# Pair counts in 256-wide items, the typed layers each in one block, the clone search moved into the first product

## The reference

```python
edge_index = jnp.stack([src, dst])
x = _layernorm(x + arma2(x, edge_index))          # L0: two ARMA convolutions of 3 stacks, batch norm, relu
x = _layernorm(x + gcn(x, edge_index))            # L1: D^-1/2 (A+I) D^-1/2 (x W) + b
x = _layernorm(x + rgcn(edge_index, edge_type_9, x))   # L2: below, two layers
x = _layernorm(x + (segment_sum(x[src], dst) @ W_neigh.T + b_neigh) + (x @ W_self.T + b_self))   # L3
# L2, per layer:
agg = segment_sum(output[srcs], seg, 2 * R * n).reshape(2 * R, n, -1)   # seg: (type, direction, node)
hidden = output @ W[-1] + b[-1]
for r in range(R):
    for inv in (0, 1):
        s = r + R * inv
        hidden = 2.0 * (hidden + agg[s] @ W[s] + count[s] * b[s]) / cnt[s]
```

## Time and profile before

| | |
|---|---|
| median of 3 runs | 4263.36 us (4261.74 to 4271.8) |
| profiled execution | 4261.65 us, span 4260.4 us |
| PE | 3151.3 us busy, 74% of the span |
| PEld | 2507.9 us, 59% |
| DVE | 2177.2 us, 51% |
| POOL | 1996.6 us, 47% |
| ACT | 1410.3 us, 33% |
| DMA | 572.7 MB moved, mean 134 GB/s |

### The profile page before, as it was taken

The page is one execution under the profiler, slowest core; times in us unless marked ns, Lnnn a source line. Parts: engine busy times, 40 slices in busy tenths (PEclk is TensorE's granted clock), DMA queues, the critical chain, the costliest instruction groups (busy, mean ns, idle before and its releaser), DMA issues. The chain is left out here.

```text
span 4260.4 us, 54185 instructions
## 1 busy us (share of the span) xinstructions
PE 3151.3 (74%) x15552; PEld 2507.9 (59%) x15554; DVE 2177.2 (51%) x3834; ACT 1410.3 (33%) x2732; POOL 1996.6 (47%) x2227
## 2 busy tenths in 40 slices
PE   6878665899999799998966878767683544444459
PEld 3545322779999596996735767655552533333348
DVE  8979996425544651556655555434363422222224
ACT  5949575556666663665200000000000000000015
POOL 4727221111111010110276777777756777777751
PEclk8989898999999899999985565555586855555559
DMA  4000156558888392984562222222263222222226
GB/s 168 5 1 1 51 200 200 204 191 293 290 290 286 136 309 92 315 286 175 197 235 67 54 54 53 53 53 54 53 242 122 53 53 53 53 53 53 53 67 209
DMA packets 170983, 572.68 MB, mean 134 GB/s; under 512 B 54368, under 2 KB 63937, under 8 KB 170380
## 3 DMA queue, kind: packets, MB, share of 16 engines
q1 hardware_dynamic: 90838, 396.53, 27.1%
q0 software_dynamic: 79536, 172.73, 14.0%
q10 hardware_dynamic: 390, 0.60, 0.0%
HBM read 405.92 MB, written 163.77 MB: 134 GB/s over the span
## 5 line engine op out<-in xcount | busy, mean ns | idle before, releaser
L2070 PE MATMUL ps_sum_rgcn<-gathered_rgcn,select_sum_rgcn 128*128 x3328 | 971.1, 439 | 570.3 <-SPq L1961 513.5
L2070 PEld LDWEIGHTS ps_sum_rgcn<-gathered_rgcn,select_sum_rgcn 128*128 128x128 f32 x3328 | 760.3, 307 | 637.0 <-issue 635.5
L1650 PE MATMUL ps_sum_arma<-pair_counts_f_sum_arma,parts_sum_arma 128*128 128x448 f32 (+1 forms) x3850 | 852.3, 373 | 14.3 <-ACT pair_counts_f_sum_arma L1691 13.6
L1986 POOL DMA_INDIRECT gathered_rgcn<-by_dst,row x782 | 739.1, 945 | 238.3 <-issue 214.9
L1650 PEld LDWEIGHTS ps_sum_arma<-pair_counts_f_sum_arma,parts_sum_arma 128*128 128x128 f32 x3850 | 708.3, 190 | 68.4 <-issue 15.1
L1986 POOL DMA_INDIRECT gathered_rgcn<-by_src,row x558 | 527.3, 945 | 199.4 <-issue 156.0
L2107 ACT COPY acc_rgcn<-ps_sum_rgcn 128x128 f32<-128x128 f32 x100 | 26.6, 266 | 1640.3 <-PE ps_sum_rgcn L2070 1640.3
L1529 POOL DMA_DIRECT2D rows<-parts_sum_arma x275 | 152.5, 555 | 884.9 <-DVE parts_sum_arma L1738 840.6
L2144 DVE TENSOR_TENSOR select_sum_rgcn<-one_hot_sum_rgcn,ps_coef_sum_rgcn 128x2048 f32<-128x2048 bf16 x52 | 118.9, 2287 | 575.6 <-PE ps_sum_rgcn L2070 575.5
L531 POOL DMA_INDIRECT scattered_rows<-record_sorts,to_row_sorts x254 | 244.0, 960 | 191.0 <-POOLq L199 114.2
L1995 PE MATMUL ps_turn_sum_rgcn<-ident,one_hot_sum_rgcn 128*128 128x128 bf16 x832 | 244.3, 301 | 79.3 <-DVE one_hot_sum_rgcn L2116 51.6
(11 more groups left out here) (466 smaller groups left out, 5132.5 us busy)
## 6 DMA issues: line engine op xcount, KB each, us to landing
blocks_arma_mid<-pairs SPq DMA_DIRECT2D x125, 800.0 KB, 6.3
axT_arma<-pairs SPq DMA_DIRECT2D x100, 800.0 KB, 6.2
pair_counts_arma_sum<-pairs SPq DMA_DIRECT2D x50, 800.0 KB, 6.2
rows<-parts_sum_arma POOLq DMA_DIRECT2D x275, 128.0 KB, 5.5
by_src<-rows_rgcn_tables SPq DMA_DIRECT2D x50, 576.0 KB, 3.8
by_dst<-rows_rgcn_tables SPq DMA_DIRECT2D x50, 576.0 KB, 3.6
exact<-whole_pairs SPq DMA_DIRECT2D x25, 800.0 KB, 3.3
pairs<-whole_pairs POOLq DMA_DIRECT2D x25, 800.0 KB, 5.2
```

Of the source, the lines that this page charges most:

```text
L1650: last = nc.tensor.matmul(ps[:, g, 0:here.stop - here.start], half(part), counts[:, n % 2, here].bitcast(F32R), start=t == 0 and part == 0 ...
L1986: nc.gpsimd.indirect_dma_start(got[:, n % PLACES, :], None, table, bass.IndirectOffsetOnAxis(ap=o.row[:, n % C:n % C + 1], axis=0)).then_i ...
L2070: nc.tensor.matmul(ps[:, bass.ds(slot, P)], select[:, parity, u, :], rows[:, bass.ds(place, D)], start=False, stop=False, skip_group_check ...
```

## The change

- *Load.* x is loaded under its own semaphore, which the ranking's SP waits for before its fill of `by_src`; only the last tile of x is zeroed; the stores of blank rows move from SP's to ScalarE's queue; `row_of` is written by VectorE; the iotas `steps` and `spare_row` move to GpSimd in the ranking.
- *Staircase.* Blocks of 256 targets (REACH), 13 a tile, 728 items, three rounds of 128 blocks; the limits are worked out for rooms of four blocks. The heavy and clone search goes. SP stores `dinv_loop` here, and the block waits for it.
- *Pair counts.* TensorE's loop is written out; it loads 16 registers per fourteen items and waits per seven; VectorE waits per eight. ScalarE casts and clears 1024 columns, a clear right after its own cast. The block waits for no store; SP fetches the first four tiles of the half counts into the ring of the first product, whose buffers and the output buffers lie in a stage around both.
- *First product.* Four tiles are fetched before; later fetches wait for the tile's store. The heavy nodes are found on VectorE at tile 2, the clone rows at tile 4, the marks in five parts at tiles 5 to 9, the nodes at tile 11; GpSimd gathers the clone rows after storing its row 11, when all count stores have landed; the subtraction is at tile 14, the factors start at tile 14.
- *Typed layers.* Tables and sum stand in one block (and layer 0's turn back in layer 1's block). Table rows and the sum's select, turned and mine buffers share SBUF, the PSUM banks are shared; VectorE waits for all table stores before its first select; GpSimd's gathers run on without EARLY, and wait for all tables at the first row of the second. SP loads the next layer's weights behind the tables.

The diff, cut to its core:

```diff
@@ load_stage
-            nc.vector.memset(k.xcur[:, :, :], 0.0).then_inc(zeroed, 1)
-            nc.vector.memset(k.row_of[:, :, :], 0.0).then_inc(cleared, 1)
+            nc.vector.memset(k.xcur[:, NT - 1, :], 0.0).then_inc(zeroed, 1)
+            nc.vector.memset(k.row_of[:, :, :], 0.0)
...
+            for first in (0, LOW):
+                here = slice(first, first + NT)
+                nc.vector.tensor_copy(k.row_of[here, :, :], k.ident16[here, here, None].to_broadcast([NT, NT, P]))
@@ rank_stage
+            @block.gpsimd
+            def _(gp):
+                nc.gpsimd.iota(k.steps[:, :, :], [[1, C], [0, 2]], base=0, channel_multiplier=0,
...
+                sp.wait_ge(k.x_loaded, 32)
@@ pair_counts_stage
             for n in range(ITEMS):
-                dve.wait_ge(multiplied, n + 1)
+                if n % EIGHT == 0:
+                    dve.wait_ge(multiplied, n + EIGHT)
...
-            with pe.Fori(0, ITEMS // BODY) as i:
...
+            for n in range(ITEMS):
+                if n % FOURTEEN == 0:
+                    table = load(PE, item_at, n // FOURTEEN * ROW, ROW, (RUNS - 1) * REACH)
+                    frees = [value & COUNTS for value in table[FOURTEEN:ROW]]
+                if n % SEVEN == 0:
+                    pe.wait_ge(made, n + SEVEN)
+                    pe.wait_ge(freed, frees[n % FOURTEEN // SEVEN])
+                    nc.tensor.nop(nofuse=True)
+                nc.tensor.matmul(ps[:, bass.ds(table[n % FOURTEEN], REACH)], source[:, n // V % 2, n % V // 2, :, n % 2],
+                                 target[:, n % V, :], start=False, stop=False, skip_group_check=True).then_inc(multiplied, 1)
...
-                    if i or g:
-                        clear(i * SPANS + g - 1)
+                    if i < NT - 1:
+                        clear(i * ROOMS + g)
...
-            for n in (0, 1):
-                sp.wait_ge(stored[n], 16 * len(range(n, NT, 2)))
-                sp.wait_ge(kept[n], 16 * len(range(n, NT, 2)))
+                if J <= i < J + FETCHED:
+                    n = i - J
+                    sp.wait_ge(kept[n % 2], 16 * (n // 2 + 1))
+                    sp.dma_start(ring[:, n, :], halves[n * P:n * P + P, :]).then_inc(k.prefetched, 16)
@@ dense_stage
+                    if exact is not None and t == NODED:
+                        gp.wait_ge(noded, 1)
+                        for n in (0, 1):
+                            gp.wait_ge(k.exact_kept[n], 16 * len(range(n, NT, 2)))
+                            gp.wait_ge(k.kept[n], 16 * len(range(n, NT, 2)))
...
+                if exact is not None and n == READY:
+                    heavy_nodes()
+                if exact is not None and n == COUNTED:
+                    clone_rows()
+                if exact is not None and FILLED <= n < FILLED + TURNS:
+                    clone_marks(n - FILLED)
+                if exact is not None and n == NODED:
+                    clone_nodes()
+                if exact is not None and n == RESTED:
                     dve.wait_ge(k.cloned, 32)
@@ typed_tables_stage, typed_sum_stage -> typed_layer_stage
-            gp.wait_ge(tiled, NT)
-            for n in range(BEHIND, EARLY):
-                gather(n)
...
+            gp.wait_ge(tiled, NT)
+            for n in range(BEHIND, TOTAL * U):
                 if not fetched(n):
                     continue
+                if n == C:
+                    gp.wait_ge(tiled, TILES)
...
+            for j in range(J):
+                dve.wait_ge(stored[j], 16 * (TILES // J))
@@ rgcn_layer
-        for layer, xT in ((0, k.xT[:, :]), (1, hidden)):
-            typed_tables_stage(nc, k, f"rgcn_tables{layer}", xT, [dram["by_src"], dram["by_dst"]], got, acc)
-            typed_sum_stage(nc, k, f"sum_rgcn{layer}", typed, got, acc, layer == 0,
-                            loads=() if layer else typed_loads(k, A, 1))
-            turn_back_stage(nc, k, f"rgcn_back{layer}", acc, hidden, ACT.Copy if layer else ACT.Relu)
+        typed_layer_stage(nc, k, "sum_rgcn0", k.xT[:, :], tables, got, acc, True, loads=typed_loads(k, A, 1))
+        typed_layer_stage(nc, k, "sum_rgcn1", hidden, tables, got, acc, False, turned_from=ACT.Relu)
+        turn_back_stage(nc, k, "rgcn_back1", acc, hidden, ACT.Copy)
```

More of the change, by code:

```diff
@@ L1037, in staircase_stage, with _ @@
         block = c.block()
+        @block.sync
+        def _(sp):
+            with nc.allow_non_contiguous_dma(reason="one value per node"):
+                sp.dma_start(loop.rearrange("(t p) o -> p (t o)", p=P), k.dinv_loop[:, :]).then_inc(looped, 16)
+            sp.wait_ge(looped, 16)
         @block.gpsimd
         def _(gp):
-            nc.gpsimd.iota(after_iota[:, :], [[1, P]], base=1, channel_multiplier=0,
-                           allow_small_or_imprecise_dtypes=True)
             nc.gpsimd.iota(at[:, :], [[1, ITEMS]], base=0, channel_multiplier=0,
@@ L1078, in _ @@
             last.then_inc(laid, 1)
-            pe.wait_ge(reached, 1)
-            nc.tensor.matmul(ps[0:1, 4, P:P + U], row[:, :], k.ident[0:U, 0:U], start=True, stop=True).then_inc(lined, 1)
-            pe.wait_ge(cloned, 1)
-            for t in range(NT):
-                last = nc.tensor.matmul(ps[:, 5, 2 * LOW:2 * LOW + 2], clone[:, t, :], place[:, t, :], start=(t == 0),
-                                        stop=(t == NT - 1))
-            last.then_inc(placed, 1)
         @block.scalar
@@ L1659, in _ @@
                         last.then_inc(used, 1)
+                if exact is not None and n == COUNTED - 1:
+                    pe.wait_ge(ready, 1)
+                    nc.tensor.transpose(ps[0:U, 7, 0:P], lane_rows[:, :], k.ident[:, :])
+                    nc.tensor.matmul(ps[:, 7, TWO_P:TWO_P + NT], ones[:, :], heavy16[:, :], start=True, stop=True)
+                    nc.tensor.matmul(ps[:, 7, TWO_P + LOW:TWO_P + LOW + NT], before[:, :], heavy16[:, :], start=True,
+                                     stop=True).then_inc(counted, 1)
+                if exact is not None and n == NODED - 1:
+                    pe.wait_ge(filled, 1)
+                    nc.tensor.matmul(ps[0:1, 7, P:P + U], row[:, :], k.ident[0:U, 0:U], start=True, stop=True)
+                    for u in range(NT):
+                        last = nc.tensor.matmul(ps[:, 7, TWO_P + 2 * LOW:TWO_P + 2 * LOW + 2], clone[:, u, :], place[:, u, :],
+                                                start=(u == 0), stop=(u == NT - 1))
+                    last.then_inc(placed, 1)
                 if loops and t < NT - 1:
@@ L1687, in _ @@
                     head(m)
[L1688 removed]
+                wait_streamed(act, n)
                 if n >= 2:
```

545 lines of the change are left out of this document (284 added, 261 removed).

## The result

The changed kernel takes 4298.94 us (median of 4 runs, 4292.98 to 4302.73) against 4263.23: ratio 1.0078, interval 1.0061 to 1.0096. It is slower by 0.8%; the forecast was 4223, 1% faster, range 4202 to 4250. The profiled execution took 4302.73 us, 41.1 more than that of before.

| stage | before | after | difference | forecast |
|---|---|---|---|---|
| load | 14.3 | 13.0 | -1.3 | -4.5 |
| first ranking | 34.8 | 39.4 | +4.6 | +4.5 |
| first sort | 174.0 | 184.1 | +10.1 | 0 |
| its end | 7.4 | 8.6 | +1.2 | 0 |
| degrees and second sort | 191.1 | 191.0 | 0.0 | 0 |

The account below looks back on a forecast made before the run. No engine was above 74% busy, so waits at block ends were taken as the bound. Typed layers -30.4, pair counts -1, first product -9, staircase +1 and load 0 took 4261.65 to 4222, stated as 4223 us; range 4202 to 4250.

Parts of the forecast that it names:

- The typed layers: Both layers: one block removes GpSimd's switch gaps and its waits for the sum's matmuls, -30.4 us, bounds -22 to -34.
- the second wait: Layer 0's sum: GpSimd's 9.00 us wait for matmuls, expected to vanish; its return would leave the typed layers at -22.
- The first product: First product: 14.6 us of waits and stall go, about 6 us of clone search is exposed; -9, bounds -15 to -4.
- Staircase: Staircase: a third threshold round, more columns and longer picks, less the clone chain and eight tail steps; +1 us.
- Load and ranking: Load and first ranking: load gains 3 to 6 us, iotas cost the ranking 0 to 5.2; net 0, bounds -6 to +5.
- Pair counts: Pair counts: narrower compares gain nothing, TensorE adds 6.4 us, the tail saves 7.5; together -1, bounds -15 to +21.
- VectorE's new wait: Pair counts: once in eight compares VectorE waits for matmuls at least eight back, with nothing behind but compares; no cost given.
- a whole register load: Pair counts, TensorE: the shortest pause, 0.84 us, was read as holding a full load; 1.0 us was taken per fourteen matmuls.
- The prediction's own sign of being wrong: Pair counts: a pause over 1.8 us per fourteen matmuls was named among the signs that would show the forecast wrong.
- Rival 4: Pair counts: written-out TensorE at half clock, pauses over 2 us per fourteen; 262 us there, 4276 in all; chance 0.04.
- The tail: End of pair counts: without waiting for stores, last compare to next block falls from 13.1 to about 5.6 us, -7.5.
- The clock: Pair counts, TensorE: granted clock between 0.55 and 0.95; 200 us at full, 218 at half, the middle 209 taken, +6.4.

## Why the prediction was wrong

- *The typed layers* (-30.4): right in mechanism and size, -33.2. The gaps gone give 30.4 between the first and the last gather of the layers (999.1 to 978.9 and 988.7 to 978.5), where 29.4 was said, and the switch 2.5 where 1.0 was said. The feared return of the second wait did not come.
- *The first product* (-9): right, -9.5; the stall came at tile 14 as placed, and its 5.67 us are near the 6 that were taken for all that was added. (The 4.27 and 10.60 that go make 14.9, not 14.6.)
- *Staircase* (+1): 1.1 came, but by luck: the terms that the prediction lists add up to 2.2. *Load and ranking* (0): the iota's price right (4.6), the load's gain 1.3 where 4.5 was taken, because VectorE's two copies took 3.47 us each, the upper end of their bounds. *ARMA*: nothing, as said.
- *Pair counts* (-1): +58.0, and so 59 of the 76 us between the forecast and the median. This is the step that failed: "So at full clock VectorE bounds (194.5 and about half of the old 10 us of stalls, 200), at half TensorE (52 x 3.98 = 207 and the old stalls, 218)." VectorE's own time was near (203 us of work), and so were TensorE's matmuls (14 x 0.19); its load was not (next point). But the sum took the larger of the two engines, which holds only while the buffers between them cover the longest pause. It said of VectorE's new wait that nothing but compares is behind it; it did not ask how far ahead VectorE may be. Before, VectorE could be 16 compares of 0.262 us ahead, 4.2 us, item by item, and the longest step over a load was 3.4 us. After, a compare is 0.201 us and the wait leaves 8 to 16 ahead, 1.6 to 3.2 us, against steps of up to 3.65 us. The two then partly add: 5.05 us per fourteen, where 3.74 or 3.98 was said. Finer waits, 32 buffers or no load bring the stage from 274 to 231, 220 and 215.
- The pause itself was mis-sized: 0.84 us was read as "a whole register load", and 1.0 taken. Over the 47 loads of the kernel before, the steps from one dozen to the next were 0.21 to 3.40 us, median 1.69; in each the needed compare had ended 1.3 us or more before, so none of them was a wait for VectorE. One row stood for a distribution, and it stood for the loads without a store in flight. The prediction's own sign of being wrong, a pause over 1.8 us per fourteen, came: 2.0 on average. The Trainium skill, "Runtime: NRT & Kernel Launch", section "Instruction fetch mechanics", gives some 200 ns per register for the loads of registers that it describes, those of the runtime; an estimate from it for 16 registers is 3.2 us. The traces don't bear this out as a price of these loads: 16 registers took 0.21 to 3.40 us before and 0.83 to 3.65 after.
- Rival 4 (a pause over 2 us per fourteen at half clock, 4276 or more) had 0.04 and was nearest. That first to last matmul take 262.5 us, its very number, is luck: of the 2.0 us per load step that match its 2.05 almost a third are waits for VectorE, and the steps between batches of seven that make up the rest are not in its sum. It blamed the written-out program; with 512-wide items the loop was no faster, and the written-out program with 32 buffers took 220, so writing out is not what made it.
- *The tail*: 10.4 us from the last compare to the next block, where 5.6 was said: the 6.4 us after the last issue were taken for the stores' landing, and they stay without that wait; what ends them no row names, and it stays open.
- *The first sort*: no step had it. The forecast costed ScalarE's copies as removed from the load and did not ask what else their first instruction carried: the table load, 10.1 us in the sort.
- The clock: the middle of the prices at full and at half was taken, 0.61 came, near the slow end. With 32 buffers, the same matmuls and less standing, it was 0.84.

## What to carry to other kernels

Where two engines meet at a ring, compare the longest pause of one with the time that the other may run ahead (buffers given out times the time of one), not their mean rates; shrinking the items or making the waits coarser shrinks that time. Before you move an engine's first instruction, look what the compiler had put in front of it. Read a pause as a distribution over all its places, never by its shortest row, and sort the places by what else was under way. Check a releaser that a row names against the time at which its work ended.

## What the runs showed of the hardware

- TensorE's steps over a load of 16 registers, where neither VectorE nor a cleared room ended them, took 0.83 to 0.96 us with no DMA packet of the stage in flight and 1.17 to 3.65 with one (the change, 11 and 22 steps). No run tests the link by leaving out the stores.
- A load of registers from a table with rows of 15 words made TensorE's step over a load up to 7.1 us; with rows and loads of 16 words it was up to 3.4 and 4.0, and the pairs took 102 and 109 us less (312.9 to 211.0, 333.6 to 224.2). With 14 words it was up to 6.0, with no kernel to compare that differs by the words alone; the 256-wide kernels, with 16 words, reached 4.8. Whether the length or the start of a row does it was not separated.
- An activation-table load of 1.28 us stood in each of the twelve turns of the sort's loop, once the loop held ScalarE's first activation; one 128x1 copy ahead of the loop took all twelve away (184.1 to 174.7 us).
- A GpSimd iota of 4.66 us held a 400-wide int32 tensor_scalar of VectorE from 0.37 to 4.85 us, but not its 3.47 us copies.
- The granted clock in the pairs, one number per kernel: 0.50 with half the columns, 0.61 in the change, 0.76 with waits per compare, 0.77 without loads, 0.84 and 0.77 with 32 buffers, 0.93 with 512 columns and 16-word rows, 0.95 before. It did not set the time of the stage: 215 us came at 0.77 and 220 at 0.84.
